# Cross attention's weights turned by DMA as two 16-bit planes, with the division moved behind the product with the values

## The reference

```python
x = x + self_attention_0(norm(x))          # 16 heads of 8, causal
x = x + cross_attention_0(norm(x), ctx)    # 8 heads of 64, + bias
x = x + quantised_ffn(norm(x))             # ternary weights, integer activations
x = x + self_attention_1(norm(x))          # 16 heads of 8, scores clipped, causal
x = x + cross_attention_1(norm(x), ctx)    # 16 heads of 64
x = x + mixture_of_8_experts(norm(x))      # gates under 0.1 dropped
```

```python
q, k, v = norm(x) @ Wq, ctx @ Wk, ctx @ Wv            # split into heads of 64
w = softmax(q @ k.T)                                  # 128 queries x 128 keys for each head
out = concat_heads(w @ v) @ Wo
```

## Time and profile before

| | |
|---|---|
| median of 3 runs | 499.45 us (499.38 to 499.49) |
| span of the profiled execution | 497.5 us, granted clock of TensorE 1.000 |
| runs' median less that span | 1.95 us |
| instructions | 15713 |
| PE / PEld busy | 98% / 84% |
| ACT / DVE / POOL busy | 88% / 80% / 75% |

### The profile page before, as it was taken

The page is one execution under the profiler, slowest core; times in us unless marked ns, Lnnn a source line. Parts: engine busy times, 40 slices in busy tenths (PEclk is TensorE's granted clock), DMA queues, the critical chain, the costliest instruction groups (busy, mean ns, idle before and its releaser), DMA issues.

```text
span 497.5 us, 15713 instructions
## 1 busy us (share of the span) xinstructions
PE 488.7 (98%) x5510; PEld 416.8 (84%) x5510; DVE 400.1 (80%) x906; ACT 437.1 (88%) x1180; POOL 371.4 (75%) x455
## 2 busy tenths in 40 slices
PE   8999999999999999999999999999999999999996
PEld 4778887888888888889889888888888898988885
DVE  5767778897888888989898898878898687876665
ACT  5988889999998898998898898989789899989782
POOL 2876677897868887788768886976869688568754
PEclk9999999999999999999999999999999999999999
DMA  6800000000000000000000000000000000000000
GB/s 196 336 2 1 3 1 3 1 2 3 1 3 1 7 2 9 1 3 7 7 3 1 8 3 5 4 7 1 4 7 1 8 7 3 7 3 2 7 7 16
DMA packets 6460, 8.64 MB, mean 17 GB/s; under 512 B 1392, under 2 KB 4848, under 8 KB 6384
## 3 DMA queue, kind: packets, MB, share of 16 engines
q1 hardware_dynamic: 5952, 6.86, 4.1%
q10 hardware_dynamic: 432, 0.79, 0.5%
HBM read 6.50 MB, written 1.05 MB: 15 GB/s over the span
## 4 chain that ended last, share of the span: by engine, by line
PE 90%; ACT 4%; DVE 2%; SPq 1%; issue 1%; DMA 1%; POOL 1%; DVEq 0%; POOLq 0%; ACTq 0%
PE psum L1270 14%; PE psum L1257 10%; PE psum L1297 10%; PE psum L1213 8%; PE psum L1335 8%; PE psum L1244 6%; PE psum L1283 3%; PE psum L1461 3%; PE psum L1347 3%; PE psum L1308 2%; PE psum L1285 2%; PE psum L1316 2%; PE psum L1310 2%; PE psum L1318 2%; PE psum L1317 2%; PE psum L1309 2%
## 5 line engine op out<-in xcount | busy, mean ns | idle before, releaser
L723 POOL TENSOR_TENSOR w_self<-w_self 128x1024 f16<-128x1024 f32 x64 | 121.2, 1901 | 27.3 <-ACT w_self L794 13.8
L805 ACT ACTIVATE w_cross<-psum,row_max_cross 128x128 f32<-128x128 f32 x384 | 104.4, 408 | 5.5 <-DVE row_max_cross L980 4.6
L728 POOL TENSOR_TENSOR w_cross<-w_cross,e_rec_cross 128x1024 f32<-128x1024 f32 x48 | 91.0, 1898 | 20.6 <-DVE e_rec_cross L989 20.6
L980 DVE TENSOR_REDUCE row_max_cross<-psum 128x8 f32<-128x1024 f32 x48 | 58.0, 1215 | 13.6 <-PE psum L1257 12.8
L987 DVE TENSOR_REDUCE e_sum_cross<-w_cross 128x8 f32<-128x1024 f32 x48 | 58.2, 1213 | 4.5 <-ACT w_cross L805 4.2
L1257 PE MATMUL psum<-kT_cross,qT_cross 64*128 64x128 f32 x768 | 54.4, 283 | 0.0
L1297 PEld LDWEIGHTS psum<-w_cross,v_cross 128*64 128x64 f32 x768 | 41.1, 136 | 14.3 <-issue 11.0
L813 ACT ACTIVATE w_cross<-psum 128x1024 f32<-128x1024 f32 x48 | 49.9, 1043 | 3.3 <-PE psum L1270 3.2
L1257 PEld LDWEIGHTS psum<-kT_cross,qT_cross 64*128 64x128 f32 x768 | 46.3, 187 | 6.8 <-issue 4.9
L1297 PE MATMUL psum<-w_cross,v_cross 128*64 128x128 f32 x768 | 51.4, 278 | 0.3 <-ACT w_cross L813 0.3
L1270 PE MATMUL psum<-ident,w_cross 128*128 128x128 f32 x384 | 49.8, 274 | 0.1
(11 more groups left out here) (213 smaller groups left out, 1377.0 us busy)
## 6 DMA issues: line engine op xcount, KB each, us to landing
out_dram<-x_all SPq DMA_DIRECT2D x16, 64.0 KB, 1.6
x_all<-in_x SPq DMA_DIRECT2D x1, 768.0 KB, 7.2
cT_all<-in_ctx SPq DMA_DIRECT2D x1, 768.0 KB, 9.4
e_k<-in_e_k SPq DMA_DIRECT2D x1, 512.0 KB, 4.9
e_v<-in_e_v SPq DMA_DIRECT2D x1, 512.0 KB, 5.8
e_q<-in_e_q SPq DMA_DIRECT2D x1, 512.0 KB, 8.6
e_o<-in_e_o SPq DMA_DIRECT2D x1, 512.0 KB, 9.5
m_w<-in_m_w SPq DMA_DIRECT2D x1, 512.0 KB, 8.5
```

What stands on the lines that cost most here:

```text
L723: pool.tensor_tensor(L.w_low[u], L.w[u][:], halves(L.w[u][:]), ALU.subtract)\
L728: pool.tensor_tensor(L.diff[u][:].rearrange("p (h k) -> p h k", h=UNIT), L.e[u][:].rearrange("p (h k) -> p h k", h=UNIT), L.e_rec[:, u, :] ...
L805: last = act.activation(L.e[u][:, P * p:P * (p + 1)], S_[:, P * p:P * (p + 1)], ACT.Exp, bias=L.row_max[:, u, p:p + 1])
L980: dve.tensor_reduce(L.row_max[:, u, :], group(i, turn)[:].rearrange("p (h k) -> p h k", h=UNIT), AX_X, ALU.max, negate=True).then_inc(L.ma ...
```

## The change

The weights of the cross attentions no longer go through PE to be turned. `ex` writes `e` as before. ACT then copies it to a 16-bit plane (`hi`), and POOL writes what is left, `e` less that plane, as a second 16-bit plane (`lo`), in place of the product with the reciprocals. SP issues one DMA transpose for each plane (`dh` after `hi`, `dm` after `lo`), from SBUF to SBUF, 128x1024 of 2 bytes each. PE's `pv` now has the turned weights stationary: for each head three 16-bit products (high plane by high values, high by low, low by high), over 65 or 64 columns, of which the 65th is a column of ones that yields the sum of the row. The result, queries by features in two PSUM banks, is divided by the sums on DVE (`nr`), and 4 transposes of float32 on PE (`T`) give the form that `oTe` copies. `rc`, `nz`, `t` and `wT` are gone. The values are kept as two 16-bit parts: ACT's `ve` writes the high part and DVE's new `vl` the low part. POOL sets the columns of ones once.

The strings of all engines are written anew, SP's too: it now holds 96 turns and the 16 stores in one order. In 13 of the 48 units it has `dm` ahead of `dh`. `AHEAD` goes from 8 and 6 to 6 and 4. One of the two buffers of `x_bias` shares its place with `f_w`. Of the many lines of `ORDER`, the two that the prediction quotes from stand here; `bg` is `cross0.s1.0` and `bn` is `cross0.pv.0`.

```diff
-AHEAD = dict(cross0=8, cross1=6)
+AHEAD = dict(cross0=6, cross1=4)
 EARLY = 4
+TURN, TURN_TAIL = 1200, 1200
...
-            fill(f"{L}.v.{c}", 695, [*context, f"{v_w}.lo"], f"{L}.ve.{c}", [ago(f"{L}.pv.{c}", AHEAD[L])])
+            fill(f"{L}.v.{c}", 695, [*context, f"{v_w}.lo"], f"{L}.vl.{c}", [ago(f"{L}.pv.{c}", AHEAD[L])])
             add(f"{L}.ve.{c}", "ACT", 484, [f"{L}.v.{c}"])
+            add(f"{L}.vl.{c}", "DVE", 605, [f"{L}.ve.{c}"])
...
-            add(f"{L}.s1.{c}", "PE", 893, [f"{L}.qe.{c}", second(f"{L}.ke.{c}")], [f"{L}.t.{c}"], "S", f"{L}.ex.{c}")
-            add(f"{L}.mx.{c}", "DVE", 1130, [f"{L}.s1.{c}"])
-            add(f"{L}.ex.{c}", "ACT", 2060, [f"{L}.mx.{c}"], [f"{L}.pv.{c}"], half=1030)
-            add(f"{L}.rc.{c}", "DVE", 1401, [f"{L}.ex.{c}"])
-            add(f"{L}.nz.{c}", "POOL", 1856, [f"{L}.rc.{c}"])
-            add(f"{L}.t.{c}", "PE", 874, [f"{L}.nz.{c}"], (), "S", f"{L}.wT.{c}")
-            add(f"{L}.wT.{c}", "ACT", 914, [f"{L}.t.{c}"])
-            fill(f"{L}.pv.{c}", 873, [f"{L}.wT.{c}", f"{L}.ve.{c}"], f"{L}.oTe.{c}", [f"{L}.{'yz'[c]}"])
-            add(f"{L}.oTe.{c}", "ACT", 486, [f"{L}.pv.{c}"])
+            add(f"{L}.s1.{c}", "PE", 893, [f"{L}.qe.{c}", second(f"{L}.ke.{c}")], (), "S", f"{L}.ex.{c}")
+            add(f"{L}.mx.{c}", "DVE", 1130, [f"{L}.s1.{c}"], [f"{L}.ex.{c}"])
+            add(f"{L}.ex.{c}", "ACT", 2060, [f"{L}.mx.{c}"], [f"{L}.lo.{c}"], half=1030)
+            add(f"{L}.hi.{c}", "ACT", 940, [f"{L}.ex.{c}"], [f"{L}.dh.{c}"])
+            add(f"{L}.dh.{c}", "SP", TURN, [f"{L}.hi.{c}"], [f"{L}.T.{c}"], tail=TURN_TAIL)
+            add(f"{L}.lo.{c}", "POOL", 1856, [f"{L}.hi.{c}"], [f"{L}.dm.{c}"])
+            add(f"{L}.dm.{c}", "SP", TURN, [f"{L}.lo.{c}"], [f"{L}.T.{c}"], tail=TURN_TAIL)
+            add(f"{L}.pv.{c}", "PE", 740, [f"{L}.dh.{c}", f"{L}.dm.{c}", f"{L}.vl.{c}", "ones"], (), "S", f"{L}.nr.{c}")
+            add(f"{L}.nr.{c}", "DVE", 930, [f"{L}.pv.{c}"])
+            fill(f"{L}.T.{c}", 437, [f"{L}.nr.{c}"], f"{L}.oTe.{c}")
+            add(f"{L}.oTe.{c}", "ACT", 486, [f"{L}.T.{c}"], [f"{L}.{'yz'[c]}"])
...
+    add("moe.out", "SP", 60, ["moe.o"])
...
+        "bKaMa0bga2bna5bAa7bpbCa5bUbraPbcaIbWbebGbYbKaVbIbna7ccaRbNbpbgbAceaYbCcgcibrbUctaMbGaKbWbKa0aIbIa2bY"
+        "bnbNbpcca7cpcebccgb4cibrb0bActb0bCcAb2b7bUcraPbWbGb2cEbYcCbeaRaKbIcFaVbgccbAa5cAbCcgaYbNaMb7a0bKcCce"
...
-        self.v = [self.sb(f"v{b}", [P, heads, XD]) for b in range(AHEAD[name])]
+        self.v_high = [self.sb(f"v_high{b}", [P, heads, XD + 1], BF16) for b in range(AHEAD[name])]
+        self.v_low = [self.sb(f"v_low{b}", [P, heads, XD], FP16) for b in range(AHEAD[name])]
         self.kT = [self.sb(f"kT{b}", [P, heads // 2, 2, P]) for b in range(AHEAD[name] // 2)]
         self.qT = self.sb("qT", [P, heads // 2, P])
-        self.e = self.diff
-        self.e_sum = self.sb("e_sum", [P, self.units, UNIT])
+        self.e = self.w
+        self.e_parts = [self.sb(f"e_parts{u}", [P, 2 * UN], FP16) for u in range(self.units)]
+        self.eT = [self.sb(f"eT{u}", [P, 2 * UNIT, P], FP16) for u in range(self.units)]
+        self.attn = [e[:].rearrange("p h q -> p (h q)").bitcast(F32)[:, 0:UNIT * XD] for e in self.eT]
...
-            for i in range(NSEQ):
+            def turn_high(L, i, u):
+                sp.wait_ge(L.e_high[u], i + 1)
+                if i:
+                    sp.wait_ge(x_full, full(i - 1, f"{L.name}.T.{u}"))
+                sp.dma_start_transpose(L.eT[u][:, 0:UNIT, :], L.e_parts[u][:, 0:UN]).then_inc(L.high_turned[u], 16)
+            def turn_low(L, i, u):
+                sp.wait_ge(L.e_low[u], i + 1)
+                if i:
+                    sp.wait_ge(x_full, full(i - 1, f"{L.name}.T.{u}"))
+                sp.dma_start_transpose(L.eT[u][:, UNIT:2 * UNIT, :], L.e_parts[u][:, UN:2 * UN])\
+                    .then_inc(L.e_turned[u], 16)
+            def store(i):
                 sp.wait_ge(*emptied(i, "moe.b"))
                 sp.dma_start(out[i], x_all[:, i, :]).then_inc(stored, 16)
...
-            def divide_by_sum(L, i, u):
-                pool.wait_ge(L.rec_ready[u], i + 1)
-                pool.tensor_tensor(L.diff[u][:].rearrange("p (h k) -> p h k", h=UNIT),
-                                   L.e[u][:].rearrange("p (h k) -> p h k", h=UNIT),
-                                   L.e_rec[:, u, :].unsqueeze(2).broadcast_to([P, UNIT, P]), ALU.mult)\
-                    .then_inc(L.diff_ready[u], 1)
+            def low_weights(L, i, u):
+                pool.wait_ge(L.e_high[u], i + 1)
+                if i:
+                    pool.wait_ge(L.e_turned[u], 16 * i)
+                pool.tensor_tensor(L.e_parts[u][:, UN:2 * UN], L.e[u][:], L.e_parts[u][:, 0:UN], ALU.subtract)\
+                    .then_inc(L.e_low[u], 1)
...
-            def weights_by_key(L, i, u):
-                turn = f"{L.name}.t.{u}"
-                act.wait_ge(s_full, score(i, turn))
-                act.activation(L.w[u][:], group(i, turn)[:], ACT.Copy).then_inc(taken(i, turn)[0], 1)
+            def high_weights(L, i, u):
+                act.wait_ge(*taken(i, f"{L.name}.s1.{u}"))
+                if i:
+                    act.wait_ge(L.high_turned[u], 16 * i)
+                act.activation(L.e_parts[u][:, 0:UN], L.e[u][:], ACT.Copy).then_inc(L.e_high[u], 1)
...
-            def reciprocal_sums(L, i, u):
-                dve.wait_ge(*taken(i, f"{L.name}.s1.{u}"))
-                if i:
-                    dve.wait_ge(L.diff_ready[u], i)
-                dve.tensor_reduce(L.e_sum[:, u, :], L.e[u][:].rearrange("p (h k) -> p h k", h=UNIT), AX_X, ALU.add)
-                dve.drain()
-                dve.reciprocal(L.e_rec[:, u, :], L.e_sum[:, u, :]).then_inc(L.rec_ready[u], 1)
+            def low_values(L, i, u):
+                buffer, heads = i % AHEAD[L.name], slice(UNIT * u, UNIT * (u + 1))
+                dve.wait_ge(L.v_made[u], i + 1)
+                dve.tensor_tensor(L.v_low[buffer][:, heads, :],
+                                  bank(i, f"{L.name}.v.{u}").rearrange("p (h w) -> p h w", w=XD),
+                                  L.v_high[buffer][:, heads, 0:XD], ALU.subtract)\
+                    .then_inc(emptied(i, f"{L.name}.v.{u}")[0], 1)
+            def divide_by_sums(L, i, u):
+                name = f"{L.name}.pv.{u}"
+                sums = by_head(group(i, name))
+                rec = L.e_rec[:, u, :].rearrange("p (z h) -> p z h", z=2)
+                dve.wait_ge(s_full, score(i, name))
+                dve.reciprocal(rec, sums[:, :, :, XD])
+                dve.drain()
+                dve.tensor_tensor(L.attn[u].rearrange("p (z h w) -> p z h w", z=2, w=XD), sums[:, :, :, 0:XD],
+                                  rec.unsqueeze(3).broadcast_to([P, 2, UNIT // 2, XD]), ALU.mult)\
+                    .then_inc(taken(i, name)[0], 1)
...
                 pe.wait_ge(*emptied(i, f"{L.name}.v.{c}"))
-                pe.wait_ge(*taken(i, f"{L.name}.t.{c}"))
+                pe.wait_ge(L.high_turned[c], 16 * (i + 1))
+                pe.wait_ge(L.e_turned[c], 16 * (i + 1))
                 room(i, name)
-                v = L.v[i % AHEAD[L.name]]
-                for h in range(UNIT * c, UNIT * (c + 1)):
-                    rows, pair = slice(XD * (h % 2), XD * (h % 2 + 1)), h % UNIT // 2
-                    last = pe.matmul(bank(i, name)[rows, P * pair:P * (pair + 1)], v[:, h, :],
-                                     L.w[c][:, P * place(h):P * (place(h) + 1)], start=True, stop=True)
+                v_high, v_low, out_ = L.v_high[i % AHEAD[L.name]], L.v_low[i % AHEAD[L.name]], group(i, name)
+                for h in range(UNIT):
+                    e_high, e_low = L.eT[c][:, place(h), :], L.eT[c][:, UNIT + place(h), :]
+                    at = 512 * (h // 4) + (XD + 1) * (h % 4)
+                    pe.matmul(out_[:, at:at + XD + 1], e_high, v_high[:, UNIT * c + h, :], start=True, stop=False)
+                    pe.matmul(out_[:, at:at + XD], e_high, v_low[:, UNIT * c + h, :], start=False, stop=False)
+                    last = pe.matmul(out_[:, at:at + XD + 1], e_low, v_high[:, UNIT * c + h, :], start=False, stop=True)
+                last.then_inc(s_full, 1)
+            def turn_attn(L, i, name, c):
+                pe.wait_ge(*taken(i, f"{L.name}.pv.{c}"))
+                room(i, name)
+                for k in range(4):
+                    last = pe.transpose(bank(i, name)[:, P * k:P * (k + 1)], L.attn[c][:, P * k:P * (k + 1)], ident[:])
                 last.then_inc(x_full, 1)
```

More of the change, by code:

```diff
@@ L31, with __init__ @@
 BANKS = 8
-AHEAD = dict(cross0=8, cross1=6)
+AHEAD = dict(cross0=6, cross1=4)
 EARLY = 4
+TURN, TURN_TAIL = 1200, 1200
 WARM = 9
 class Step:
-    def __init__(self, engine, cost, after, again, bank, until, parts, once, half, first, last):
+    def __init__(self, engine, cost, after, again, bank, until, parts, once, half, first, last, tail):
+        self.tail = TAIL[engine] if tail is None else tail
```

(11 more changed lines are left out.)

174 lines of the change are left out of this document (103 added, 71 removed).

## The result

The changed kernel takes 519.4 us, the kernel before 499.5 in the same comparison: ratio 1.038, 95% interval 1.036 to 1.041. It is 3.8% slower, where 470 us and "faster" were forecast. The profiled execution has a span of 517.8 us.

What follows compares the result with a forecast made beforehand. PE, 98% busy, was taken as the bound, so its saving would come off the span: 497.5 - 38.5 + 5 + 1 + 3 = 468, or 470 us as time; range 457 to 492, held at 0.8.

Steps and rivals of the forecast that it cites:

- what PE loses and gains: On PE, `t` (0.87 us) and old `pv` (1.03) go, `T` (0.44) and new `pv` (0.70) come: 0.76 saved a unit, 36.5 in all.
- The 2 us for change-overs: On PE, the array's change-over ahead of the old `pv` goes: 2 us saved, bounds 0 to 7.
- The rival of slow 16-bit products: In PE's new `pv`, the 24 products run at 54 ns each: 492 to 499 us; chance 0.04.
- the queue of turns: Rival: the DMA transposes' own queue, through the DMA engines or SP, becomes the bound: about 700 us; chance 0.09.
- "+3" for nearly level engines: PE, ACT and DVE, nearly level in fixed order, lose some time to each other: 3 us taken from 0 to 18.
- the 38.5 in the sum: The whole saving forecast on PE: 36.5 us over 48 units and 2 for change-overs.
- stalls "+5": At `pv` on PE, waits for both turned planes: eight units lack 11 us together, partly shared, counted as 5.
- `lo` at 1.90: POOL's subtraction `lo` takes 1.90 us, as self attention's does, replacing `nz` (1898 ns) at no added cost.
- a turn at 2.8: A plane's DMA transpose lands 2.8 us after its issue, bounds 1.6 to 5.1.
- The late-turns rival: DMA transposes land late, at 5.1 us, and `pv` waits: 483 to 495 us; chance 0.12.
- +1 for the end: After the last `pv`, `nr` and `T` stand where only `oTe` did: 1 us more.
- ACT as the bound: Rival: ACT, needing 437 us, takes over from PE as the limit: 477 to 487 us; chance 0.17.

## Why the prediction was wrong

**Right: what PE loses and gains.** From start to start a unit saves 0.73 us (0.76 taken): `pv` 0.73 (0.70 taken), `T` 0.44. The 2 us for change-overs no run separates. `hi` 1.10, DVE 406.7 (408), ACT 438.9 (437). The rival of slow 16-bit products is out, and so is the queue of turns: a turn would have had to hold the DMA engines or SP for 4.8 us; SP is held 1.23, and with the turns issued but not read nothing is lost. The 1309 ns that the Trainium skill gives in "VectorE: DVE Perf Modes", section "The three transpose paths", for 128x128 by the DMA crossbar do not add up block after block: eight blocks land together after 3.2 us. The advice of the Trainium skill on the same page, section "Rules for kernel authors", to use TensorE where PSUM will do as the target fares better: the turns do cost time here, 20.8 us in the changed kernel's lists and 5.9 in an order made for them. Still, with such an order and a split `pv` the kernel with DMA turns is 1.3% faster than the one that turns on TensorE.

**Wrong: "+3" for nearly level engines.** This is the step that failed. I took 3 out of 0 to 18, by the stretch in which PE lost nothing with ACT 9% behind the earlier trace rows. But that row shows lists in which PE is the longest and everybody else waits for it; it says nothing of lists in which PE has become 8% shorter. A saving on PE alone of 53 us by starts, more than the change's, brought 10.5 us. If the change's own brings no more, then of the 38.5 in the sum at least 28 are lost again, an estimate from that run: the term stood at 3, and its bounds of 0 to 18 were too low as well. The row that could have warned stands in the earlier trace rows: 489, 437, 400 and 371 us, and chains of `mx`, `ex`, the sums and `nz` through three engines for each unit, whose length PE's saving does not touch.

**Wrong: stalls "+5".** They were summed by holding each unit's chain against the work that stands between `s1` and `pv` in PE's list, each unit by itself, with `lo` at 1.90 and a turn at 2.8. Both were longer, 0.24 and 0.4 us in the median, and each start in the chain waits for its own engine's list too, as in the example above, where POOL's and SP's lists added 0.7 and 0.3 us; the turn itself, one of the longest, landed 4.7 us after its issue. Waiting for turns costs 20.8 us in these lists (without turns: 498.6). The late-turns rival had the mechanism right, with 483 to 495, and counted it on top of a PE gain that was not there.

**Wrong: `lo` at 1.90.** 2.14; with turns that is worth 2.6 us, without 1.8. I took the row of self attention's subtraction, whose two operands lie in one tile; the operand that differed was not looked at.

**The sum by the runs.** From 499.4 the run with PE alone lighter comes to 488.9: 10.5 off. The changed kernel without turns and with `lo` at 1.90 stands at 496.8, +7.9: a smaller saving on PE (35 us by starts, not 53), DVE's 7 us, a smaller `AHEAD`, other lists; which of these, no run separates, and the prediction had +1 for the end. `lo`'s 0.24: +1.8. The turns: +20.8. That is 519.4. And the order takes 21 of it back, the split of `pv` another 5. The 1.8 is no larger than the spread of single times.

**ACT as the bound** did not happen either: it was never over 46 of 50 us in the changed kernel's stretches above. What took over from PE was no single engine but the chains between them, in the changed kernel most of all through POOL (38% of the chain). The prediction had no rival for that on the slower side.

**The chance.** Faster had 0.88. Each rival was priced as if it stood alone on top of PE's saving, and so all but the queue of turns ended at 499 or below. One run of the kernel before with a lighter PE would have shown that the saving was worth some 10 us in its lists, and any loss above that a slower kernel.

## What to carry to other kernels

An engine at 98% is the bound only as far as the next chain. Here, with four engines between 75% and 98% in fixed lists, a saving of 53 us on the longest brought 10.5. Lay the lists out again for the new durations: that brought the changed kernel 21 us. But don't count on the whole saving even then: without turns and with lists that fit it stood 7 us below the kernel before. Make only the bound cheaper, in the old kernel and whatever it then computes, before paying anything for the saving: it costs a few lines and shows what the saving is worth. And where an engine in order waits for two things, let it start on the one that is there; half a microsecond at `pv` was worth 5 to 9 us here.

## What the hardware did that was not expected

- A DMA transpose of 128x1024 16-bit elements from SBUF to SBUF lands 3.2 us after its issue; one of 128x512 after 2.5. The issue holds SP's queue for 1.23 to 1.28 us (medians) for either size, three times a plain load's 0.43.
- A subtraction of 128x1024 on POOL, float32 in, 16 bits out, takes 2.14 us if the second operand is a separate float16 plane and 1.89 if it is the upper half of the first, read as bfloat16.
- The granted clock fell to 0.50 (1.2 GHz) for some microseconds after PE had stood still for 2.19 us; with PE's pauses filled its mean stayed at 0.996 and more, and the kernels were not faster for it.
